# Cross attention on one core: whole float32 exponentials, the bias on GpSimd, and new orders of work

## The reference

```python
Q = (x @ w_q.T)          # x: 8 batches x 1024 rows x 512
K = (ctx @ w_k.T); V = (ctx @ w_v.T)      # ctx: 8 batches x 64 keys x 512
# 16 heads of 32
scores = einsum('bhqd,bhkd->bhqk', Q, K) / sqrt(32)
attn = softmax(scores, axis=-1)
c = einsum('bhqk,bhkd->bhqd', attn, V)    # heads back to 512 columns
z = c @ w_o.T + b_o + x
out = (z - mean(z)) * rsqrt(var(z) + 1e-5) * gamma + beta
```

## Time and profile before

| | |
|---|---|
| median of 3 runs | 613.3 us (612.41 to 617.44) |
| profiled execution | 616.87 us, of it 615.10 us span |
| mean granted TensorE clock | 0.977 |
| busy: PE, DVE, ACT, POOL | 582.4, 472.7, 450.3, 476.6 us |

### The profile page before, as it was taken

One profiled execution on the slowest core, in us unless ns is written; L12 is line 12 of the kernel. 1 busy time (PEld: TensorE's weight loads), 2 busy tenths in 40 slices (PEclk: granted clock), 3 DMA queues, 4 the chain that ended last, 5 costly groups with the idle time before them and its releaser, 6 DMA issues.

```text
span 615.1 us, 12235 instructions
## 1 busy us (share of the span) xinstructions
PE 582.4 (95%) x4330; PEld 462.0 (75%) x4330; DVE 472.7 (77%) x874; ACT 450.3 (73%) x799; POOL 476.6 (77%) x333
## 2 busy tenths in 40 slices
PE   8888889998999999999999999998999999999875
PEld 7655558887877888788868788886888877888553
DVE  7857348876888888888868888886888877888657
ACT  7657467867877788888777888885888777877831
POOL 4627347886988888988878888897789888878840
PEclk9989889998999999999989999998999999999988
DMA  8342213332343333433334233333334423122323
GB/s 308 126 91 58 57 42 96 95 91 92 114 116 87 114 103 104 121 115 91 102 97 120 85 109 113 102 115 88 100 104 118 114 84 93 55 71 74 108 85 120
DMA packets 79757, 62.74 MB, mean 102 GB/s; under 512 B 52272, under 2 KB 52272, under 8 KB 79696
## 3 DMA queue, kind: packets, MB, share of 16 engines
q1 hardware_dynamic: 79696, 61.96, 33.9%
HBM read 39.39 MB, written 16.78 MB: 91 GB/s over the span
## 4 chain that ended last, share of the span: by engine, by line
PE 81%; DVE 6%; ACT 4%; DMA 4%; issue 3%; SPq 1%; POOL 1%; ACTq 0%; DVEq 0%
PE ps_q L425 23%; PE ps_o L431 23%; PE ps_c L473 13%; PE ps_s L368 6%; DMA out<-y 4%; PE ps_o L393 3%; PE ps_o L307 3%; PE ps_s L307 3%; PE ps_s L379 3%; PE ps_q L307 2%; SPq L287 1%; ACT inverse L582 1%; DVE q_lo L634 1%; DVE turned L721 1%; DVE half_max L727 1%
## 5 line engine op out<-in xcount | busy, mean ns | idle before, releaser
L817 POOL TENSOR_TENSOR p_lo<-probs,p_hi 128x1024 fp32r<-128x1024 f32 x59 | 142.2, 2410 | 67.3 <-ACT p_hi L515 67.3
L425 PE MATMUL ps_q<-x_hi,wq_lo 64*128 64x512 f32 x448 | 179.1, 400 | 6.2 <-DVE q_lo L634 6.2
L431 PE MATMUL ps_o<-wo_hi,c_lo 64*128 64x512 f32 x448 | 179.1, 400 | 0.0
L431 PE MATMUL ps_o<-wo_lo,c_hi 64*128 64x512 f32 x448 | 178.2, 398 | 0.0
L425 PE MATMUL ps_q<-x_lo,wq_hi 64*128 64x512 f32 x448 | 177.4, 396 | 0.0
L425 PE MATMUL ps_q<-x_hi,wq_hi 64*128 64x512 f32 x448 | 176.9, 395 | 0.0
L431 PE MATMUL ps_o<-wo_hi,c_hi 64*128 64x512 f32 x448 | 176.8, 395 | 0.0
L425 PEld LDWEIGHTS ps_q<-x_hi,wq_lo 64*128 64x128 f32 x448 | 83.5, 186 | 17.8 <-DVE q_lo L634 10.5
L721 DVE STREAM_TRANSPOSE turned<-ps_s 128x1024 f32<-128x1024 f32 x64 | 80.0, 1251 | 14.1 <-PE ps_s L368 9.8
L431 PEld LDWEIGHTS ps_o<-wo_lo,c_hi 64*128 64x128 f32 x448 | 84.0, 188 | 8.4
L425 PEld LDWEIGHTS ps_q<-x_hi,wq_hi 64*128 64x128 f32 x448 | 83.8, 187 | 8.6
(11 more groups left out here) (123 smaller groups left out, 1436.2 us busy)
## 6 DMA issues: line engine op xcount, KB each, us to landing
xT_raw<-in_xT SPq DMA_DIRECT2D x64, 256.0 KB, 3.0
x_raw<-in_x SPq DMA_DIRECT2D x64, 256.0 KB, 2.9
out<-y SPq DMA_DIRECT2D x64, 256.0 KB, 2.2
max_rows<-max_turned SPq DMA_DIRECT2D x128, 16.0 KB
ctx_raw<-in_ctxT SPq DMA_DIRECT2D x4, 256.0 KB, 5.0
wk_raw<-in_wkT SPq DMA_DIRECT2D x4, 256.0 KB, 5.3
wq_raw<-in_wqT SPq DMA_DIRECT2D x4, 256.0 KB, 6.0
wv_raw<-in_wvT SPq DMA_DIRECT2D x4, 256.0 KB, 7.3
```

Source lines behind the costliest of these rows:

```text
L425: return nc.tensor.matmul(ps_q[:, 0, :], w[l][half, k, dims], x_[r][half, qc % 2, k, :], start=(half is lower and k == 0 and step == 0), s ...
L431: return nc.tensor.matmul(ps_o[:, 0, :], cx[l][half, k, tile], wo[r][half, k, :], start=False, stop=(half is lower and k == KT - 1 and ste ...
L817: nc.gpsimd.tensor_tensor(p_lo[:, :, :], probs_of(n)[:, :, :], p_hi[:, :, :].bitcast(fp32), ALU.subtract).then_inc(p_lo_done, 1)
```

## The change

- The exponentials are not split. `probs` has two buffers, the values are kept whole in `values` (no block-diagonal copies and no DMAs for them), and `combine_values` is one call of eight float32 matmuls, each a 64x32 tile of the array: two halves of rows (the head) by four groups of columns (values or ones, pair). Each streams 512 columns.
- In a full step these eight come before `subtract_max`, in one piece.
- The bias is added to `x_raw` by GpSimd (`add_bias`); `start_output` is gone, and `project_both` itself waits for `z` of the tile before.
- `shift` moves from VectorE to GpSimd. `y` has four buffers instead of two.
- The maxima use all 128 partitions: VectorE folds with two instructions in place of one, `max_turned` is twice as wide, and four DMAs instead of two spread it. `select` and the keys have another layout; each batch's keys come with two DMAs in each of four steps, and those of the values are gone.
- The first copies of w_v are made by GpSimd. Steps 0 to 6 have their own orders: values' products in steps 1 to 4 (one b2 in each), VectorE takes the maxima ahead of the division, values are copied straight from PSUM by ScalarE (even batches) and VectorE (odd ones).
- The last slots and tiles have an order written out by hand on every engine; outputs alternate between two banks; only the last tile's gamma and beta are on VectorE.

```diff
-            def combine_values(n, second):
...
-                for step, (lhs, rhs) in enumerate(((vbd_lo, p_hi), (vbd_hi, p_hi), (vbd_hi, p_lo))):
-                    if not second and step == 2:
-                        pe.wait_ge(p_lo_done, n + 1)
-                    for pair in range(2):
...
+            def combine_values(n):
+
+                b, g = n // PER_BATCH, n % G
+                pe.wait_ge(exp_done, n + 1)
+                wait(pe, c_raw_done, n)
...
+                for what in range(2):
+                    for pair in range(2):
+                        for head in range(2):
+                            rows, col = slice(64 * head, 64 * (head + 1)), 64 * (what ^ head) + 32 * pair
+                            mm = nc.tensor.matmul(ps_c[col:col + DK, head, :],
+                                                  ones[rows, :] if what else values[rows, b, g, pair, :],
+                                                  probs[rows, n % 2, pair, :], start=True, stop=True)
+                mm.then_inc(c_product, 1)
...
                 if not second:
+                    if i == 0:
...
+                    wait(pe, z_done, i)
                     wait(pe, q_lo_done, n)
-                    wait_context(i)
...
             project_queries(0)
-            for t in range(SLOTS + OUT_LAG):
+            for t in range(SLOTS - 1):
                 n, i = t + 1, t - OUT_LAG
-                if n < SLOTS and i >= 0:
+                if i >= 0:
                     project_both(n, i, False)
                     score(t)
                     project_both(n, i, True)
-                    combine_values(t - 2, False)
+                    combine_values(t - 2)
                     subtract_max(t - 1)
-                    start_output(i + 1)
-                    combine_values(t - 2, True)
                     continue
...
+                score(t)
+                project_queries(n)
+                if t >= 1:
                     subtract_max(t - 1)
...
+                if 1 <= t <= KT:
+                    project_values(t - 1)
+                if t >= 2:
+                    combine_values(t - 2)
+
+
+            score(SLOTS - 1)
+            project_output(56)
+            combine_values(SLOTS - 3)
+            subtract_max(SLOTS - 2)
+            project_output(57)
+            project_output(58)
+            subtract_max(SLOTS - 1)
+            combine_values(SLOTS - 2)
+            project_output(59)
+            combine_values(SLOTS - 1)
+            for i in (60, 61, 62, 63):
+                project_output(i)
...
                     for pair in range(2):
-                        sp.dma_start(max_rows[64 * pair:64 * pair + 8, :].bitcast(fp32).rearrange(
-                            "p (b j) -> p b j", j=32), max_turned[:, :]).then_inc(max_rows_filled, 16)
+                        for part in range(2):
+                            row = 64 * pair + 8 * part
+                            sp.dma_start(max_rows[row:row + 8, :].bitcast(fp32).rearrange("p (b j) -> p b j", j=32),
+                                         max_turned[:, part, :]).then_inc(max_rows_filled, 16)
```

The full steps on ScalarE, VectorE and GpSimd after the change:

```diff
+            for t in range(OUT_LAG, SLOTS - 1):
                 i = t - OUT_LAG - 1
...
+                log_sums(t - 3)
+                negate_max(t - 1)
+                invert_sums(t - 3)
+                if i >= 0:
+                    invert_deviation(i)
                 if t + SPLIT_AHEAD < SLOTS:
                     split_x(t + SPLIT_AHEAD)
...
+                context_to_hi(t - 3)
+                if i >= 0:
+                    normalise(i)
+                queries_to_hi(t + 1)
+                exponentiate(t - 1)
...
+                turn_max(t - 1)
+                divide(t - 3)
+                turn_scores(t)
+                half_maxima(t)
+                add_residual(i)
+                queries_to_lo(t + 1)
+                fold_halves(t)
+                statistics(i)
...
+                if i >= 1:
+                    shift_mean(i - 1)
+                if t + SPLIT_AHEAD < SLOTS:
+                    split_x(t + SPLIT_AHEAD)
+                context_to_lo(t - 3)
+                if i >= 1:
+                    scale(i - 1)
+                add_bias(i + 1)
```

More of the change, by code:

```diff
@@ new lines, in normalise, with exponentiate @@
+            def normalise(i):
+                s = i % 2
+                act.wait_ge(shift_done, i + 1)
+                wait(act, y_stored[i % 4], 16 * (i // 4))
+                nc.scalar.activation(y[:, i % 4, :], z[:, s, :], ACT.Identity, bias=shift[:, s:s + 1],
+                                     scale=rstd[:, s:s + 1]).then_inc(normed_done, 1)
+            def exponentiate(n):
+                act.wait_ge(shifted_done, n + 1)
+                wait(act, c_product, n - 1)
+                nc.scalar.activation(probs[:, n % 2, :, :], ps_s[:, 2 * (n % 2):2 * (n % 2) + 2, :], ACT.Exp,
+                                     scale=SCALE).then_inc(exp_done, 1)
@@ new lines, in _ @@
+            for t in range(OUT_LAG, SLOTS - 1):
+                i = t - OUT_LAG
+                turn_max(t - 1)
+                divide(t - 3)
+                turn_scores(t)
+                half_maxima(t)
+                add_residual(i)
+                queries_to_lo(t + 1)
+                fold_halves(t)
+                statistics(i)
+            turn_max(SLOTS - 2)
+            divide(SLOTS - 4)
+            turn_scores(SLOTS - 1)
+            add_residual(56)
+            half_maxima(SLOTS - 1)
@@ new lines, in _ @@
+            fold_halves(SLOTS - 1)
+            turn_max(SLOTS - 1)
+            divide(SLOTS - 3)
+            statistics(56)
+            for i in (57, 58):
+                add_residual(i)
+                statistics(i)
+            divide(SLOTS - 2)
+            add_residual(59)
+            statistics(59)
+            divide(SLOTS - 1)
+            for i in (60, 61, 62, 63):
+                add_residual(i)
+                statistics(i)
+            i, s = TILES - 1, (TILES - 1) % 2
+            dve.wait_ge(mean_var_done, i + 1)
@@ new lines, in _ @@
+            wait(dve, y_stored[i % 4], 16 * (i // 4))
+            nc.vector.scalar_tensor_tensor(out=y[:, i % 4, :], in0=z[:, s, :], scalar=mean_var[:, s, 0:1],
+                                           in1=gamma_row[:, :], op0=ALU.subtract, op1=ALU.mult
+                                           ).then_inc(last_scaled_done, 1)
+            dve.wait_ge(rstd_done, i + 1)
+            dve.wait_ge(last_scaled_done, 1)
+            nc.vector.scalar_tensor_tensor(out=y[:, i % 4, :], in0=y[:, i % 4, :], scalar=rstd[:, s:s + 1],
+                                           in1=beta_row[:, :], op0=ALU.mult, op1=ALU.add).then_inc(last_y_done, 1)
@@ L836, in _ @@
+            for t in range(OUT_LAG):
+                split_x(t + SPLIT_AHEAD)
                 if 3 <= t < 3 + KT:
```

648 lines of the change are left out of this document (273 added, 375 removed).

## The result

The changed kernel takes 595.4 us (median of 4 runs, 594.46 to 595.56) against 615.2 for the kernel before in the same session (612.41 to 617.44): a ratio of 0.968, 95% interval 0.963 to 0.973. The profiled execution took 595.55 us, 593.8 of it span.

The account below looks back on a forecast made before the run. Prediction: a two-step chain (16.98 us) bounds full steps, with an 8.30 floor from the query copies. 95.1 early + 459.0 full steps + 44.5 end = 598.6 span, 1.77 around it: 600 us; forecast 590 to 607, 8 in 10 584 to 620.

Parts of the forecast that it names:

- The group of eight, 0.93: Values' product on TensorE: eight float32 tiles take four passes of 0.233 us, groups of columns overlapping fully, 0.93 us.
- The rivals of groups that take turns: Values' product: four column groups in turn, 3.73 us, 736 in all, chance 0.10; two at a time, 629, chance 0.06.
- The 1.33 up to the maxima: Full steps: from last matmul of `project_both` to the maxima, 0.03 + 0.24 + 0.93 + 0.13 us in place of 0.72.
- The full steps, 8.50: The 54 middle steps: 8.50 us each, 459.0 in place of 461.99.
- 16.98, a step 8.49: Two-step chain, maxima through exponentials, negation, `half_max`, `z` and `project_both`: 16.98 us over two steps, so 8.49 each.
- The floor of 8.30: Full steps: query copies chain fills the 2.02 us outside `project_both` and `score`, so no step goes below 8.30 us.
- The long steps, 13.8: Full steps where `y` waits for an earlier tile's store: 13.8 us in all, ended by four buffers of `y`.
- The four DMAs: Loop from maxima to maxima over four DMAs, which take 4.06: 7.90 us, under 8.50 with 0.6 to spare.
- The early steps: Steps with values' products before full steps: 9.3 us instead of 11.96; 8.5 us booked, stage ending at 95.1.
- The end, 44.5: Stage from the maxima of slot 61 to the end: 44.5 us in place of 49.46, bounds 41 and 50.
- GpSimd needs 3 x 1.30 + 0.2 = 4.1 a tile ... the last bias is added at about 38.3: End: GpSimd takes 4.1 us a tile against 2.8 of an output and falls behind; last bias at about 38.3.
- the last product follow output 59 at 20.5: End, counted from the maxima of slot 61: a product and output 59 bring 19.1 us, the last product 20.5.

Follow-up runs that it names:

- experiments 4: Changed kernel, full steps issue only the values' four tiles of the product, leaving out the four of the sums: 593.4 us, ratio 0.971.
- experiment 5: Changed kernel with the eight tiles of the product issued twice in full steps, the second time over the first: 619.3 us, ratio 1.011.
- experiment 1: Changed kernel with the maxima's matmuls ahead of the values' product in full steps: 589.1 us, ratio 0.965.
- Experiment 7: Kernel before with four buffers of `y` instead of two, the rest untouched: 603.3 us, ratio 0.987.
- experiment 6: Changed kernel with two buffers of `y` instead of four: 681.6 us, ratio 1.115.
- experiment 2: Changed kernel with a fifth DMA of `max_turned`, to a spare tile, issued by SP ahead of the four: 608.2 us, ratio 0.997.
- experiment 3: Changed kernel with two of the maxima's four DMAs issued by ScalarE, early steps included: 605.0 us, ratio 0.990.
- Experiment 9: Changed kernel, in GpSimd's last tiles the bias comes between `shift` and gamma: 594.5 us, ratio 0.970.
- experiment 11: Changed kernel with maxima first in full steps, GpSimd's bias between `shift` and gamma, and the last two slots ahead of outputs: 589.6 us, ratio 0.962.
- experiment 8: Changed kernel with gamma and beta of tiles 58 to 63 on VectorE and `y` of tile 56 ahead of the last exponentials: 591.0 us, ratio 0.967.

## Why the prediction was right, and where it was not

The sum was right, 600 against 595.4, and so was the sign. That the sum was this close owes something to luck, since the full steps and the end missed in opposite directions. Of its terms:

**The group of eight, 0.93.** Measured 0.90, all groups of columns beside each other; experiments 4 and 5 show that the price is in the streams and not in the number of tiles. The rivals of groups that take turns had the right question and the wrong answer. (TensorE: Matmul & The Clock Gate of the Trainium skill, Part 3, had two figures for this, which give two estimates: by the span of one matmul and 4 ns a tile 0.96, by its 10.6 times 1.4. The trace agrees with the first.) (FP8 and Floating Point Precision of the Trainium skill, TensorE Precision Notes, has four passes for true FP32; two entries of 0.45 each, against 0.233 for one fp32r pass, agree.) The 1.33 up to the maxima came out too (1.35), but its parts did not: 0.23 of it is the interval after any matmul, for which the sum had 0.03, and the two changes of tiling take about 0.22 of it, for which the sum had 0.37.

**The full steps, 8.50; measured 8.22.** The mechanism was right: experiment 1 takes the product out of the chain and leaves 8.12, by the query copies. The sizes were not, and the term that failed is "16.98, a step 8.49". Each part of it was a little too long: 1.35 to the maxima instead of 1.44 with the second change, 0.54 to the exponentials instead of 0.65, 2.51 instead of 2.52, 4.40 to `z` instead of 4.53, 1.43 instead of 1.56, 6.17 instead of 6.28. That is 16.40 for 16.98, two steps of 8.20. Some of this can be read. Experiment 7 shows TensorE busy all the time at 8.30 a step, and there `project_both` starts 0.21 after `q_lo` has ended, in the changed kernel 0.10 to 0.15: that was a wait for TensorE. And in the kernel before, the two matmuls of a pair do not start together. The second of the maxima mostly starts 0.20 to 0.24 after the first, in the changed kernel with it, which is more than the 0.12 at the exponentials. The query matmuls lose time around the scores, 1.14 us there (the rows below, of the kernel before) and 0.96 in the changed kernel, which gives the 0.11 of `project_both` together with its first interval, 0.24 before and 0.31 now.

```profile
303.08 0.39 PE L425 MATMUL ps_q<-x_hi,wq_hi 64*128 64x512 f32 x1
304.22 0.39 PE L425 MATMUL ps_q<-x_hi,wq_lo 64*128 64x512 f32 x1
```

So intervals that I took for the chain's own lengths held waits for TensorE and the uneven start of the pairs. None of this was tested by itself. The floor of 8.30, "the cover is just as long as the chain", fails too, as the steps of 8.22 and 8.12 show: where `q_lo` is the releaser, `project_both` starts 1.92 after its last matmul, not 2.02, and with 6.17 that is 8.09. Over 54 steps the 0.28 is 15.3 us.

**The long steps, 13.8.** Experiment 7 measures 13.7 for the four buffers alone, between two profiled executions. So of the 18.3 us of the stage three quarters come from the buffers, and 4.5 from the step of 8.22 instead of 8.30. What the prediction missed is that the buffers are no extra: with two of them the changed kernel is 11% slower than the one before (experiment 6). Its store leaves SP 1.3 us later than before, behind two more DMAs, and that comes on top of the 9.4 us or more that it already waited for its turn; how the loss divides among them is not shown.

**The four DMAs.** A loop of 7.90 with 0.6 to spare was forecast; experiment 2 gives about 7.8 and 0.4, experiment 3 confirms that it is no bound.

**The early steps.** 9.3 was forecast; slots 1 to 4 take 9.26 to 9.46. The stage ended at 96.37 for 95.1.

**The end, 44.5; measured 53.7.** The maxima of slots 62 and 63 came at 7.7 and 14.4 as forecast (7.9 and 14.4). Wrong is the step "GpSimd needs 3 x 1.30 + 0.2 = 4.1 a tile ... the last bias is added at about 38.3": it ended at 586.45 - 540.10 = 46.4. GpSimd has 38.66 us of work in this stage and waited for 11 more: 6.7 for `y`, which waits for the `shift` that GpSimd itself has just made, 2.7 for `c_hi`, 1.8 for `rstd`. The step that failed is the cost of a tile on GpSimd: I had costed its instructions and not the round trip through ScalarE between two of them. I had also let the last product follow output 59 at 20.5, though it needs the one bank of `ps_c`, and that the division of slot 62, which stood on VectorE behind a `z` that waited for GpSimd: it ran at 23.7. Experiment 9 shows that removing the wait for `y` gives 1.6 us, as the next wait is close behind, and experiment 11 that bringing the last slots forward gives nothing more; experiment 8, that taking work off GpSimd gives 4.9. The other 4 of the 9.2 lie, by the trace of experiment 8, in the last slot's logarithm and division, which stand behind work for the outputs, and in the low clock after the waits that follow. The forecast had neither, and no run removes them. A third buffer for `x_raw` was not tried either, and that trace gives little hope for it.

## What to carry to other kernels

A term read from a trace in which one engine is saturated can contain waits for that engine: take each link of a chain from a place where its releaser is named, or expect it to be an upper bound. An engine that issues A, lets another engine work on A's result and then consumes it costs the round trip, unless something else stands between; and in the hand-written end here moving work off the queue with the most of it gave 4.9 us, reordering it 1.6. When DMAs are added to a queue, ask whose buffers are released by what stands behind them, and how long a finished result already waits there for its turn.

## What the runs showed of the hardware

A float32 matmul of 512 columns appears as two entries of 0.61 to 0.63 us, which start 0.45 apart; eight in 64x32 tiles take as long as four (0.90 to 1.00), and sixteen 0.85 more. At the lower clock an entry takes 1.08. Of the 1.35 from the last matmul before the group to the first behind it, 0.90 is the group and 0.23 the interval after any matmul, so the two changes of tiling take about 0.22; in experiment 5 the interval after that is 0.34 (304.76 to 305.10), 0.11 more than usual. Four DMAs of 16 KB cost SP 2.57 us of issue, and an operation of 128x512 with two inputs costs GpSimd 1.26 to 1.30, where VectorE needs 0.69 for its sum and 0.73 to 1.7 for a scaling in the end. Two of these DMAs issued by ScalarE, with loads on SP's queue at the same time, were awaited until 7.0 us after their issue began (61.23 to 68.25), where the four on SP's queue are there 4.1 to 4.4 after `max_turned`.
